# Two graph attention layers: the factor row made in every partition, and the turned tiles moved ahead in the second layer

## The chip, the cores and the metric

The kernel runs on one core of a Trainium2 chip. The metric is the device time of one execution in microseconds (us); the time before is the median of three runs. All data and all matmuls are float32.

## What is computed

For each of 8 graphs with 1024 nodes and 128 features, two layers run one after the other, each on the layer-normalised input behind a relu:

```python
h = relu(layernorm(x)); x = x + gat0(h)        # gat0 ends in elu
h = relu(layernorm(x)); x = x + gat1(h)        # gat1 has no elu
# gat: Wh = h @ W; e[i, j] = leaky_relu(Wh[i] @ a1 + Wh[j] @ a2, 0.2)
#      softmax over j where adj[i, j], then the sum of softmax * Wh[j]
```

The kernel uses that the leaky relu's exponential is a product and a maximum: with c the largest `Wh @ a2` of the graph, the weight of the pair (i, j) is the larger of a factor of j alone and a factor r of i alone, up to factors that cancel in the softmax. r is exp(-0.8 * max(Wh[i] @ a1 + c, 0)). So every partition (a node j) needs the row r of all 1024 nodes i, and every graph needs its c.

## The kernel before, in words

There are 16 **stages**: stage n is layer n // 8 and graph n % 8, and the program's constant LAST is 15. A graph has T = 8 tiles of 128 nodes. The loop over n (L1090 on TensorE, L841 on VectorE, L553 on ScalarE, L296 on the DMA queue of SyncE) overlaps three stages: it attends stage n, projects stage n+1 and makes the normalised input of stage n+2. Each engine has its order written out by hand, and semaphores bind them. Turn n of the loop finishes stage n-1; "a turn with elu" is one where stage n-1 is of the first layer, n = 1 to 8, and turns 9 to 14 are without elu.

**TensorE** in turn n: `project(n + 1)` is 8 matmuls, 16 instructions (a float32 matmul is two). In even turns `usum_pair` adds two. `attend(n, ...)` is 8 tiles of 8 matmuls, 128 instructions. In the middle of tile 0 `spread_emax` (L974) sends one transpose: the largest e2 of each partition (`emax`) is turned so that each partition gets all 128 of them. `transposes(n + 2)` (L900) turns the eight normalised tiles `xn`, 8 instructions, ahead of tile 6 in a turn with elu and of tile 5 in the others.

**VectorE** in turn n: the first two masks (`masks`, L734, 1024 columns, one per tile of attend), `take_acc(n - 1)` (three copies of the sums out of PSUM and a reciprocal `rec`), `copy_e(n + 1)` (L673: e1 and e2 out of the projection, then `emax`), a mask and `exp_args` in this order, or the other in turns without elu (L695: c as `cmax`, then `zrow` = max(e1 + c, 0) and `from_max` = e2 - c), the masks up to 5, `add_elu` or `add_hp`, masks 6 and 7, `statistics(n + 3)`. The masks of the next turn wait for the row `row_r` of the next stage.

**ScalarE**: `exps(n + 1)` (r, the two factors q and s, and the column of q in `wh`), `scale_accs(n - 1)` (8 instructions), `elu_exp` where there is an elu, `normalise(n + 2)` (8 instructions into `xn`), `scale_wh(n + 1)` (8), `sort_row(n + 1)` (L478: the row in the order that the masks want), `copy_hT(n + 2)` (L437). In even turns `copy_u` (L487) copies two rows of sums. TensorE's next `project` waits for all of `scale_wh` and for `copy_hT`.

**SyncE's queue**: `load_row(n + 1)` (L251) waits for r, writes it to `row_mem` in DRAM, waits for the landing, and reads it back into all 128 partitions (`in_row`). In odd stages the two rows `u_sums` travel with it. Behind it in the same queue stand the adjacency loads (1 MB each), the loads of x and the stores.

**GpSimd** has the statistics of the normalisation (`centre`, `variance`, `normaliser`) and nothing else in the loop.

Of the kernel before, what the change touches and what calls it, by code (L numbers as in the profile page):

```python
# [5 lines left out]
P = 128  # L6
# [6 lines left out]
SLOPE = 0.2  # L13
# [5 lines left out]
def gat_two_layers(nc, x, adj, w0, w0t, a0, w1, w1t, a1, r_rows, out):  # L19
# [27 lines left out]


# [6 lines left out]
    with ExitStack() as ctx:  # L55
# [36 lines left out]
        ecol = sb("ecol", [P, T, 2])  # L92
        emax = sb("emax", [P, 1])
# [6 lines left out]
        in_row = sb("in_row", [P, N + 2 * C])  # L100
        row_by_node = in_row[:, 0:N]
        u_rows = in_row[:, N:N + 2 * C].rearrange("p (s c) -> p s c", s=2)
# [16 lines left out]
        row_mem = nc.dram_tensor("row_mem", (N + 2 * C,), F32, kind="Internal").ap()  # L119
# [56 lines left out]
        q_ready = sem("q_ready")  # L176
        row_sorted = sem("row_sorted")
# [42 lines left out]

        def written(m):

            return loaded_rows(m) + (m - 1) // 2
# [14 lines left out]
        def _(sp):  # L238
# [11 lines left out]

            def load_row(m):  # L251
                k = loaded_rows(m)
                if m % 2 == 1:

                    sp.wait_ge(u_copied, m // 2)
                    sp.wait_ge(row_in, 16 * (k - 1))
                    sp.dma_start(row_mem[N:N + 2 * C].rearrange("(s c) -> s c", s=2),
                                 u_sums[:, :]).then_inc(r_written, 16)

                sp.wait_ge(r_known, m + 1)  # L260
                if k > 1:
                    sp.wait_ge(row_in, 16 * (k - 1))
                sp.dma_start(row_mem[0:N].rearrange("(p t) -> p t", t=T),
                             sqr[:, m % 2, 2, :]).then_inc(r_written, 16)
                sp.wait_ge(r_written, 16 * written(m))
                if k > 1:
                    sp.wait_ge(row_sorted, k - 1)

                sp.wait_ge(acc_copied, NB * (m - 1))
                if m % 2 == 0:  # L270
                    sp.dma_start(row_by_node, row_mem[0:N].partition_broadcast(P)
                                 ).then_inc(row_in, 16)
                else:
                    sp.dma_start(in_row[:, :], row_mem.partition_broadcast(P)).then_inc(row_in, 16)
# [42 lines left out]
        def _(pool):  # L317
# [34 lines left out]

            nc.gpsimd.memset(ident[:, :], 0.0).then_inc(const_set, 1)
# [14 lines left out]
            for m in range(1, LAST + 1):  # L368
                if m != 2:
                    centre(m)  # L370
                    variance(m)
                normaliser(m)

        @block.scalar
        def _(act):
# [71 lines left out]
            def exps(m):  # L447

                act.wait_ge(z_ready, m + 1)
                nc.scalar.activation(sqr[:, m % 2, 2, :], zrow[:, :], ACT.Exp,  # L450
                                     scale=SLOPE - 1.0).then_inc(r_known, 1)
                act.wait_ge(args_ready, m + 1)
                nc.scalar.activation(sqr[:, m % 2, 1, :], from_max[:, :], ACT.Exp,
                                     scale=SLOPE).then_inc(q_known, 1)
                nc.scalar.activation(sqr[:, m % 2, 0, :], from_max[:, :], ACT.Exp,
                                     scale=1.0 - SLOPE).then_inc(sqr_ready, 1)
                if m > 0:
                    act.wait_ge(q_known, m + 1)
                    nc.scalar.mul(wh[:, m % 2, :, D], sqr[:, m % 2, 1, :],
                                  Q_SCALE).then_inc(q_ready, 1)  # L460

# [16 lines left out]
            def sort_row(m):  # L478

                k = loaded_rows(m)  # L480
                act.wait_ge(row_in, 16 * k)
                act.wait_ge(p_ready, T * (m - 1))
                nc.scalar.activation(row_r[:, m % 2, :].rearrange("q (t p) -> q t p", t=T),  # L483
                                     row_by_node[:, :].rearrange("q (p t) -> q t p", t=T),
                                     ACT.Copy).then_inc(row_sorted, 1)

            def copy_u(n):  # L487
                k = n // 2
                act.wait_ge(upair_done, k)
                if k > 1:  # L490
                    act.wait_ge(r_written, 16 * written(n - 1))
                nc.scalar.activation(u_sums[:, 0:D], UPAIR, ACT.Copy,  # L492
                                     scale=EMPTY).then_inc(u_copied, 1)
# [59 lines left out]
            for n in range(1, LAST + 1):  # L553
                elu = stages[n - 1][0] == 0
                if n == LAST:
                    seed_last()
                if n < LAST and not elu:
                    if n % 2 == 0:
                        copy_u(n)
                    exps(n + 1)  # L560
                scale_accs(n - 1)
                if n < LAST:
                    if elu:
                        if n % 2 == 0:
                            copy_u(n)
                        exps(n + 1)
# [5 lines left out]
                    early = T // 2 if elu else T  # L572
                    scale_wh(n + 1, range(early))
                    sort_row(n + 1)
                    if early < T:
                        scale_wh(n + 1, range(early, T))
                if n + 2 <= LAST:
                    copy_hT(n + 2)

        @block.vector  # L580
        def _(dve):
# [103 lines left out]

            def exp_args_first():
# [8 lines left out]
            def exp_args(m):  # L695
                dve.wait_ge(emax_spread, m + 1)
# [41 lines left out]
            def mask_unsorted(n):  # L738
# [6 lines left out]
                    row_by_node[:, :].rearrange("q (p t) -> q t p", t=T),  # L745
# [95 lines left out]
            for n in range(1, LAST):  # L841
# [3 lines left out]
                copy_e(n + 1)  # L845
                if l == 0:
                    masks(n, (DRAIN,))
                    exp_args(n + 1)
                else:

                    exp_args(n + 1)
                    masks(n, (DRAIN,))
                masks(n, range(DRAIN + 1, 6))
# [19 lines left out]
        def _(pe):  # L873
# [26 lines left out]
            def transposes(m):  # L900
# [5 lines left out]
                else:  # L906
                    pe.wait_ge(cmax_ready, m)
# [82 lines left out]
            def spread_r(m):  # L990
                pe.wait_ge(r_known, m + 1)
# [98 lines left out]
            for n in range(1, LAST):  # L1090
# [4 lines left out]
                k = 6 if stages[n - 1][0] == 0 else 5  # L1095
                attend(n, (0,), emax_of=n + 1)
# [37 lines left out]
```

## Time and profile before

| what | value |
|---|---|
| median of 3 runs | 290.97 us (290.93 to 291.45) |
| the profiled execution | 291.18 us |
| its span, first to last instruction | 289.4 us |
| TensorE busy | 285.1 us (99%) |
| VectorE busy | 254.4 us (88%) |
| ScalarE busy | 195.1 us (67%) |
| GpSimd busy | 79.7 us (28%) |
| HBM traffic | 291 GB/s over the span |

The span leaves out some 1.8 us around the program. An engine is busy while one of its instructions runs; TensorE's instructions overlap each other, so that the distance from one start to the next tells more than their length. A row of the timeline has start, length, engine, line, operation, tiles, count, and in brackets the idle time ahead of it and who ended it.

### The profile page before, as it was taken

Reading aid. Unit: us, or ns where it says so; the run is one execution under the profiler, and the core shown is the slowest. Engines: PE = TensorE matmul, PEld = TensorE weight load, DVE = VectorE, ACT = ScalarE, POOL = GpSimd, SP = SyncE. Lnnn points to the kernel's source line nnn. Section 1 sums busy time; section 2 is a strip of 40 time slices with the busy share of each in tenths; the row PEclk is TensorE's granted clock in tenths of the full one; section 3 lists DMA queues with packets and bytes.
Section 4 is the critical chain, followed back from the end, with each engine's and each line's share of the span. In section 5 each row is a group of like instructions: output and inputs, shape, how many; then the busy total and the mean of one; then the engine's idle time right before and its main releaser. Section 6 shows DMA issues by size and latency. Waiting matters only on the chain.

```text
span 289.4 us, 6600 instructions
## 1 busy us (share of the span) xinstructions
PE 285.1 (99%) x2523; PEld 284.2 (98%) x2523; DVE 254.4 (88%) x493; ACT 195.1 (67%) x534; POOL 79.7 (28%) x143
## 2 busy tenths in 40 slices
PE   7999999999999999999999999999999999999996
PEld 7999999999999999999999999999999999999995
DVE  3898899898989989898998979979797997779986
ACT  4686795995959679495886929569292865916400
POOL 2412705315071420706035070512407042000000
PEclk9999999999999999999999999999999999999999
DMA  7999659597795949679287896959769596896922
GB/s 235 418 407 407 243 183 408 216 371 298 260 413 163 415 170 359 278 245 412 76 315 286 291 378 204 404 186 389 294 243 410 166 409 250 313 406 205 374 104 75
DMA packets 25387, 84.52 MB, mean 292 GB/s; under 512 B 3966, under 2 KB 5132, under 8 KB 25356
## 3 DMA queue, kind: packets, MB, share of 16 engines
q1 hardware_dynamic: 24780, 83.70, 76.8%
q8 instruction: 20, 0.33, 0.4%
q10 hardware_dynamic: 576, 0.39, 0.4%
q14 instruction: 11, 0.09, 0.1%
HBM read 79.83 MB, written 4.26 MB: 291 GB/s over the span
## 4 chain that ended last, share of the span: by engine, by line
PE 99%; POOL 0%; DVE 0%; issue 0%; POOLq 0%
PE acc L1041 76%; PE prj L957 9%; PE tp L887 5%; PE acc L1056 2%; PE acc L876 2%; PE acc L937 1%; PE tp L976 1%; PE prj L1056 1%; PE prj L927 1%; PE prj L1041 1%; PE tp L970 1%; PE tp L896 0%; PE tp L993 0%; PE tp L985 0%; PE acc L896 0%
## 5 line engine op out<-in xcount | busy, mean ns | idle before, releaser
L1041 PE MATMUL acc<-wh,pbuf 128*128 128x129 f32 x1968 | 227.6, 275 | 0.0
L1041 PEld LDWEIGHTS acc<-wh,pbuf 128*128 128x128 f32 x1968 | 224.0, 192 | 0.1
L734 DVE SCALAR_TENSOR_TENSOR pbuf<-row_r,sqr,adj_sb 128x1024 f32<-128x1024 f32 x125 | 154.8, 1277 | 2.9 <-ACT row_r L483 2.9
L498 ACT ACTIVATE accs<-accs,rec 128x128 f32<-128x128 f32 x120 | 36.6, 388 | 26.7 <-DVE rec L770 26.7
L320 POOL TENSOR_TENSOR mean<-stats 128x8 f32<-128x8 f32 x14 | 11.7, 836 | 142.9 <-DVE stats L632 139.5
L433 ACT ACTIVATE xn<-x_sb,shift,rstd 128x128 f32<-128x128 f32 x120 | 47.7, 479 | 0.0
L466 ACT ACTIVATE wh<-prj,wh 128x128 f32<-128x128 f32 x120 | 32.8, 363 | 0.0
L483 ACT ACTIVATE row_r<-in_row 128x1024 f32<-128x1024 f32 x14 | 29.4, 2098 | 2.4 <-DMA in_row<-row_mem 2.4
L957 PE MATMUL prj<-w_ext,hT 128*128 128x130 f32 x240 | 29.3, 275 | 0.0
L957 PEld LDWEIGHTS prj<-w_ext,hT 128*128 128x128 f32 x240 | 28.0, 191 | 0.0
L347 POOL TENSOR_TENSOR rstd<-vareps,neg_half 128x8 f32<-128x8 f32 x15 | 26.0, 1731 | 6.9 <-DVE vareps L651 5.8
L632 DVE BATCH_NORM_STATS2 stats<-x_sb 128x6 f32<-128x128 f32 x112 | 23.0, 278 | 0.0
L450 ACT ACTIVATE sqr<-zrow 128x8 f32<-128x8 f32 x16 | 3.3, 209 | 27.3 <-DVE zrow L699 26.9
L760 DVE TENSOR_TENSOR accs<-acc,in_row 128x387 f32<-128x387 f32 (+1 forms) x39 | 18.7, 512 | 0.6 <-PE acc L1041 0.2
L676 DVE COPY ecol<-prj 128x12 f32<-128x12 f32 x15 | 2.6, 171 | 16.1 <-PE prj L957 15.4
L323 POOL TENSOR_SCALAR negmean<-mean 128x8 f32<-128x8 f32 x14 | 15.6, 1112 | 1.2
L444 ACT ACTIVATE hT<-tp 128x1024 f32<-128x1024 f32 x15 | 15.5, 1033 | 0.6 <-PE tp L887 0.6
L887 PE MATMUL tp<-ident,xn 128*128 128x128 f32 x120 | 15.6, 273 | 0.0
L887 PEld LDWEIGHTS tp<-ident,xn 128*128 128x128 f32 x120 | 13.6, 141 | 0.0
L492 ACT ACTIVATE u_sums<-tp 2x128 f32<-2x128 f32 x7 | 1.8, 257 | 13.8 <-PE tp L970 13.8
L781 DVE TENSOR_TENSOR x_sb<-x_sb,ex 128x1024 f32<-128x1024 f32 x8 | 9.7, 1217 | 0.0
L775 DVE SCALAR_TENSOR_TENSOR ex<-accs,ex 128x1024 f32<-128x1024 f32 x8 | 9.7, 1217 | 0.0
(114 smaller groups left out, 181.1 us busy)
## 6 DMA issues: line engine op xcount, KB each, us to landing
adj_sb<-in_adj SPq DMA_DIRECT2D x64, 1024.0 KB, 10.7
in_row<-row_mem SPq DMA_DIRECT2D x7, 641.0 KB, 4.3
x_sb<-in_x SPq DMA_DIRECT2D x7, 512.0 KB, 11.5
in_row<-row_mem SPq DMA_DIRECT2D x7, 512.0 KB, 4.3
out_x<-x_sb SPq DMA_DIRECT2D x7, 512.0 KB, 12.9
x_sb<-in_x ACTq DMA_DIRECT2D x1, 256.0 KB, 3.6
x_sb<-in_x SPq DMA_DIRECT2D x1, 256.0 KB, 3.5
row_mem<-sqr SPq DMA_DIRECT2D x14, 4.0 KB
```

Of the source, the lines that this page charges most:

```text
L323: nc.gpsimd.tensor_scalar(negmean[:, :], mean2[:, :], -0.5, None, ALU.mult).then_inc(pool_means, 1)
L347: nc.gpsimd.tensor_tensor(rstd[:, :], vareps[:, :], neg_half[:, :], ALU.pow).then_inc(rstd_ready, 1)
L433: nc.scalar.activation(xn[:, t, :], src[:, t, :], ACT.Identity, bias=shift[:, t:t + 1], scale=rstd[:, t:t + 1]).then_inc(xn_ready, 1)
L466: nc.scalar.activation(wh[:, m % 2, t, 0:D], prj[:, k, s * E:s * E + D], ACT.Copy, scale=wh[:, m % 2, t, D:C]).then_inc(wh_ready, 1)
L483: nc.scalar.activation(row_r[:, m % 2, :].rearrange("q (t p) -> q t p", t=T), row_by_node[:, :].rearrange("q (p t) -> q t p", t=T), ACT.Co ...
L498: op = nc.scalar.activation(hp[:, t, :], hp[:, t, :], ACT.Copy, scale=rec[:, t:t + 1])
L632: st = nc.vector.bn_stats(stats[:, t, :], src[:, t, :])
L734: nc.vector.scalar_tensor_tensor(pbuf[:, t, :], row_r[:, n % 2, :], sqr[:, n % 2, 0, t:t + 1], adj_at(n, t), ALU.max, ALU.min).then_inc(p_ ...
L760: nc.vector.tensor_tensor(accs[:, k * NB:k * NB + w, :], acc[:, k, 0:w * C].rearrange("p (s c) -> p s c", c=C), uniform_of(e).unsqueeze(1) ...
L887: return nc.tensor.transpose(tp[:, t * P:(t + 1) * P], xn[:, t, :], ident[:, :])
L957: mm = nc.tensor.matmul(prj[:, k, s * E:(s + 1) * E], hT[:, t * P:(t + 1) * P], w_ext[:, l, :], start=(s == 0), stop=True, skip_group_chec ...
L1041: mm = nc.tensor.matmul(sum_at(k, s), pbuf[:, t, i * P:(i + 1) * P], wh[:, n % 2, t, :], start=(t == 0 and s == 0 and k < NB), stop=(t == ...
```

## The change

In stages 2 to 14 the row r is no longer made once and sent: e1 of all nodes and each partition's largest e2 travel through DRAM together, nine numbers a partition instead of eight (`e_row`, a row of 1152 instead of 1024 numbers in `row_mem` and `in_row`). They leave as soon as `emax` is made. Every partition then takes c from its own copy (`exp_args_later`) and makes r for all 1024 nodes itself (`make_row`: a relu with c as its bias, then an exponential in place). c is taken ahead of mask 6 in turns with elu, ahead of mask 7 in the others. `spread_emax` stays for stages 0, 1 and 15 (`OWN_R`). The column of q moves from ScalarE to GpSimd (`last_column`), `copy_u` from ScalarE to VectorE. In turns without elu `transposes` moves from ahead of tile 5 to ahead of tile 3, and `copy_hT` from the end of ScalarE's turn to right behind `normalise`. The diff, cut to its core:

```diff
+    OWN_R = (0, 1, LAST)
+        e_pair = sb("e_pair", [P, 2, T + 1])
+        e_row = e_pair[:, 0, :]
+        e2 = e_pair[:, 1, 0:T]
+        ROW = N + P
+        row_parts = in_row[:, 0:ROW].rearrange("q (p t) -> q t p", t=T + 1)
...
             def load_row(m):
+                if m in OWN_R:
...
+                else:
+                    sp.wait_ge(emax_ready, m + 1)
+                    sp.dma_start(row_mem[0:ROW].rearrange("(p t) -> p t", t=T + 1),
+                                 e_row).then_inc(r_written, 16)
+                    if m % 2 == 1:
+                        store_uniform(m)
...
+            def last_column(m):
+                pool.wait_ge(q_known, m + 1)
+                nc.gpsimd.tensor_scalar(wh[:, m % 2, :, D], sqr[:, m % 2, 1, :], Q_SCALE, None,
+                                        ALU.mult).then_inc(q_ready, 1)
...
                 normaliser(m)
+                if m > 2:
+                    last_column(m - 1)
...
+            def make_row(m):
+                k = loaded_rows(m)
+                act.wait_ge(row_in, 16 * k)
+                act.wait_ge(cmax_ready, m + 1)
+                act.wait_ge(p_ready, T * (m - 1))
+                nc.scalar.activation(row_r[:, m % 2, :].rearrange("q (t p) -> q t p", t=T),
+                                     row_parts[:, 0:T, :], ACT.Relu,
+                                     bias=cmax[:, 0:1]).then_inc(row_added, 1)
+                act.wait_ge(row_added, k)
+                nc.scalar.activation(row_r[:, m % 2, :], row_r[:, m % 2, :], ACT.Exp,
+                                     scale=SLOPE - 1.0).then_inc(row_sorted, 1)
...
                     if n + 2 <= LAST:
                         normalise(n + 2)
+                        if not elu:
+                            copy_hT(n + 2)
+                    if n + 1 == LAST:
+                        scale_wh(n + 1)
+                        sort_row(n + 1)
+                    else:
+                        exps_later(n + 1)
+                        make_row(n + 1)
+                        scale_wh(n + 1)
-                if n + 2 <= LAST:
+                if n + 2 <= LAST and elu:
                     copy_hT(n + 2)
...
+            def exp_args_later(m):
+                dve.wait_ge(row_in, 16 * loaded_rows(m))
+                nc.vector.tensor_reduce(cmax[:, :], row_parts[:, T, :], AX_X,
+                                        ALU.max).then_inc(cmax_ready, 1)
+                dve.wait_ge(cmax_ready, m + 1)
+                nc.vector.tensor_scalar(from_max[:, :], e2, cmax[:, 0:1], None,
+                                        ALU.subtract).then_inc(args_ready, 1)
...
+                masks(n, range(DRAIN, 6))
                 if l == 0:
                     add_elu(b)
+                    exp_args_later(n + 1)
                     masks(n, (6,))
                     add_x(b)
                     masks(n, (7,))
                 else:
                     add_hp(b)
-                    masks(n, (6, 7))
+                    masks(n, (6,))
+                    if n + 1 < LAST:
+                        exp_args_later(n + 1)
+                    masks(n, (7,))
...
-                else:
-                    pe.wait_ge(cmax_ready, m)
                 pe.wait_ge(xn_ready, xn_before(m + 1))
...
-                k = 6 if stages[n - 1][0] == 0 else 5
-                attend(n, (0,), emax_of=n + 1)
+                k = 6 if stages[n - 1][0] == 0 else 3
+                attend(n, (0,), emax_of=n + 1 if n + 1 == LAST else None)
```

`copy_e_later` is `copy_e` with e1 and e2 in separate rows, so that e1 and the maximum lie together; `exps_later` is `exps` without r and without the column.

## Rows read from the trace of the kernel before

**Rows 1.** The page, part 1: busy time and share of TensorE.

```profile
PE 285.1 (99%) x2523; PEld 284.2 (98%) x2523; DVE 254.4 (88%) x493; ACT 195.1 (67%) x534; POOL 79.7 (28%) x143
```

**Rows 2.** The page, part 4: the chain of waits, share by engine.

```profile
PE 99%; POOL 0%; DVE 0%; issue 0%; POOLq 0%
```

**Rows 3.** Timeline of TensorE: turn 3 from its first instruction to turn 4's.

```profile
66.83 1.95 PE L957 MATMUL prj<-w_ext,hT 128*128 128x130 f32 x16
...
69.51 0.27 PE L976 MATMUL tp<-ident,emax 128*128 128x128 f32 x1
...
83.89 1.95 PE L957 MATMUL prj<-w_ext,hT 128*128 128x130 f32 x16
```

**Rows 4.** Timeline of turn 3 (with elu): VectorE, ScalarE and the DMA queue.

```profile
68.82 0.17 DVE L676 COPY ecol<-prj 128x12 f32<-128x12 f32 x1 [1.10 <-PE prj L957]
69.09 0.16 DVE L684 TENSOR_REDUCE emax<-ecol 128x1 f32<-128x8 f32 x1
...
70.36 0.28 DVE L697 TENSOR_REDUCE cmax<-tp 128x1 f32<-128x128 f32 x1
...
70.96 3.67 DVE L734 SCALAR_TENSOR_TENSOR pbuf<-row_r,sqr,adj_sb 128x1024 f32<-128x1024 f32 x3
...
71.18 0.34 SPq L263 DMA_DIRECT2D row_mem<-sqr  x1
...
72.93 0.34 SPq L271 DMA_DIRECT2D in_row<-row_mem  x1
...
74.55 1.21 DVE L775 SCALAR_TENSOR_TENSOR ex<-accs,ex 128x1024 f32<-128x1024 f32 x1
...
75.69 1.27 DVE L734 SCALAR_TENSOR_TENSOR pbuf<-row_r,sqr,adj_sb 128x1024 f32<-128x1024 f32 x1
...
80.63 1.06 ACT L444 ACTIVATE hT<-tp 128x1024 f32<-128x1024 f32 x1
...
81.54 0.25 ACT L444 ACTIVATION_READ_ACCUMULATOR hT<-tp 128x1 f32 x1
...
84.58 0.20 DVE L770 RECIPROCAL rec<-accs 128x8 f32<-128x8 f32 x1
```

**Rows 5.** Lines by form: line, operation, count, busy us, mean ns, idle before.

```profile
L483 ACT ACTIVATE row_r<-in_row 128x1024 f32<-128x1024 f32 x14 | 29.4, 2098 | 2.4 <-DMA in_row<-row_mem 2.4
...
L323 POOL TENSOR_SCALAR negmean<-mean 128x8 f32<-128x8 f32 x14 | 15.6, 1112 | 1.2
...
L510 ACT ACTIVATE ex<-ex 128x1024 f32<-128x1024 f32 x8 | 8.5, 1058 | 0.3
...
L453 ACT ACTIVATE sqr<-from_max 128x8 f32<-128x8 f32 x16 | 3.3, 209 | 0.0
```

**Rows 6.** The tile in_row: time from issue to landing of its reads.

```profile
DMA to landing us min/median/max: 3.6/4.3/4.5
```

**Rows 7.** Timeline of turn 11 (without elu), ScalarE and VectorE.

```profile
208.31 2.44 ACT L498 ACTIVATE accs<-accs,rec 128x128 f32<-128x128 f32 x8
...
210.75 3.18 ACT L433 ACTIVATE xn<-x_sb,shift,rstd 128x128 f32<-128x128 f32 x8
...
213.83 2.12 ACT L466 ACTIVATE wh<-prj,wh 128x128 f32<-128x128 f32 x8
...
218.04 2.48 DVE L734 SCALAR_TENSOR_TENSOR pbuf<-row_r,sqr,adj_sb 128x1024 f32<-128x1024 f32 x2 [0.25 <-ACT row_r L483]
...
221.99 0.20 DVE L770 RECIPROCAL rec<-accs 128x8 f32<-128x8 f32 x1
```

**Rows 8.** Timeline of the DMA queue: the row's write and read, turn 8.

```profile
156.95 0.35 SPq L263 DMA_DIRECT2D row_mem<-sqr  x1
...
159.21 0.33 SPq L274 DMA_DIRECT2D in_row<-row_mem  x1
```

**Rows 9.** The same in turn 13.

```profile
242.41 0.34 SPq L263 DMA_DIRECT2D row_mem<-sqr  x1
...
245.67 0.32 SPq L271 DMA_DIRECT2D in_row<-row_mem  x1
```

More of the change, by code:

```diff
@@ L98, in gat_two_layers @@
         row_r = sb("row_r", [P, 2, N])
[L100 to L102 removed]
+        ROW = N + P
+        in_row = sb("in_row", [P, ROW + 2 * C])
+        row_parts = in_row[:, 0:ROW].rearrange("q (p t) -> q t p", t=T + 1)
+        u_rows = in_row[:, ROW:ROW + 2 * C].rearrange("p (s c) -> p s c", s=2)
         uniform = sb("uniform", [P, 2, C])
@@ L219, in e_copies, with own_rows @@
             return 3 * m + 3 if m < 2 else 2 * m + 4
+        def own_rows(m):
+            return len([k for k in OWN_R if k < m])
         def written(m):
@@ L270, in load_row @@
                 if m % 2 == 0:
-                    sp.dma_start(row_by_node, row_mem[0:N].partition_broadcast(P)
+                    sp.dma_start(in_row[:, 0:ROW], row_mem[0:ROW].partition_broadcast(P)
                                  ).then_inc(row_in, 16)
@@ L460, in exps, with exps_later @@
                                   Q_SCALE).then_inc(q_ready, 1)
+            def exps_later(m):
+                act.wait_ge(args_ready, m + 1)
+                nc.scalar.activation(sqr[:, m % 2, 1, :], from_max[:, :], ACT.Exp,
+                                     scale=SLOPE).then_inc(q_known, 1)
+                nc.scalar.activation(sqr[:, m % 2, 0, :], from_max[:, :], ACT.Exp,
+                                     scale=1.0 - SLOPE).then_inc(sqr_ready, 1)
             def scale_wh(m, tiles=range(T)):
@@ L556, in _ @@
                     seed_last()
-                if n < LAST and not elu:
-                    if n % 2 == 0:
-                        copy_u(n)
+                if n + 1 == LAST:
                     exps(n + 1)
@@ L569, in _ @@
                         normalise(n + 2)
[L572 to L576, printed above, removed]
-                if n + 2 <= LAST:
+                        if not elu:
+                            copy_hT(n + 2)
+                    if n + 1 == LAST:
+                        scale_wh(n + 1)
[5 more added lines that the diff above has]
+                if n + 2 <= LAST and elu:
                     copy_hT(n + 2)
@@ L684, in copy_e, with copy_e_later, copy_u @@
                 nc.vector.tensor_reduce(emax[:, :], ecol[:, :, 1], AX_X, ALU.max).then_inc(emax_ready, 1)
+            def copy_e_later(m):
+                dve.wait_ge(prj_done, m + 1)
+                full = prj[:, 0:2, 0:NB * E].rearrange("p b (s e) -> p b s e", e=E)[:, :, :, D:E]
+                nc.vector.tensor_copy(e_pair[:, :, 0:2 * NB].rearrange("p e (b s) -> p b s e", b=2),
+                                      full).then_inc(e_copied, 1)
+                part = prj[:, 2, 0:tiles_in[2] * E].rearrange("p (s e) -> p s e", e=E)[:, :, D:E]
+                nc.vector.tensor_copy(e_pair[:, :, 2 * NB:T].rearrange("p e t -> p t e"),
+                                      part).then_inc(e_copied, 1)
+                dve.wait_ge(e_copied, e_copies(m))
+                nc.vector.tensor_reduce(e_row[:, T:T + 1], e2, AX_X,
+                                        ALU.max).then_inc(emax_ready, 1)
+            def copy_u(n):
+                k = n // 2
+                dve.wait_ge(upair_done, k)
+                if k > 1:
+                    dve.wait_ge(r_written, 16 * written(n - 1))
+                nc.vector.tensor_scalar(u_sums[:, 0:D], UPAIR, EMPTY, None,
+                                        ALU.mult).then_inc(u_copied, 1)
             def exp_args_first():
@@ L844, in _ @@
                 take_acc(n - 1)
-                copy_e(n + 1)
-                if l == 0:
-                    masks(n, (DRAIN,))
+                if n + 1 == LAST:
+                    copy_e(n + 1)
+                else:
+                    copy_e_later(n + 1)
+                if n % 2 == 0:
+                    copy_u(n)
+                if n + 1 == LAST:
                     exp_args(n + 1)
-                else:
-                    exp_args(n + 1)
-                    masks(n, (DRAIN,))
-                masks(n, range(DRAIN + 1, 6))
+                masks(n, range(DRAIN, 6))
                 if l == 0:
                     add_elu(b)
+                    exp_args_later(n + 1)
                     masks(n, (6,))
```

40 lines of the change are left out of this document (15 added, 25 removed).

## The prediction

> **What bounds the kernel now.** I read the busy shares first: TensorE is busy for 99% of the span, VectorE for 88% [rows 1]. The chain of waits says the same: 99% of what ended last is TensorE [rows 2]. Busy time of overlapping matmuls proves little, so the timeline of TensorE comes next. From the first instruction of turn 3 to that of turn 4 are 17.06 us [rows 3]. The code issues 153 instructions in it: 16 of project, 128 of attend, 8 transposes, 1 of spread_emax. That is 0.1115 us for each, and the view shows no idle time anywhere in the turn. So TensorE issues back to back: an instruction less is time less, and any wait that reaches it is time more. What the other engines have left is read from rows 4: VectorE waits 1.10 us for the projection in this turn and for nothing else, and ScalarE has hT ready at 81.79 (81.54 + 0.25), 2.1 us ahead of the project that needs it.
>
> **The change on TensorE.** One transpose goes in each of the turns 1 to 13: 13 x 0.1115 = 1.45 us. Moving the eight others from tile 5 to tile 3 changes no count. If nothing else reaches TensorE, the profiled execution goes from 291.18 to 289.73, and the median, which stands 0.21 below it, from 290.97 to 289.52. A turn is then 16.95 us, or 17.17 with the two instructions of usum_pair. The Trainium skill, page "TensorE: Matmul & The Clock Gate", section "Back-to-back issue gap", gives some 81 ns for a matmul with 128 columns; by it the 13 would be worth an estimated 1.05 us. The row's 0.1115 decides, since it is this kernel's own spacing.
>
> **The row's way, with elu.** I count from T, the first instruction of a turn (66.83 in turn 3). In turn 3 emax is done at 69.25, T + 2.42 [rows 4]. The write left at 71.18, behind the spread, three VectorE operations and an exponential. Now it leaves at T + 2.42, 1.93 us earlier. From the write to the read's issue are 1.75 us in turn 3 [rows 4], and the read lands 4.3 us after its issue [rows 6]. So the row is there at T + 8.47. The broadcast carries 64 KB more on its 512 or 641 KB; both old sizes have the same median to landing, so I add nothing. The adjacency loads stand behind the row in the same queue and start earlier by as much; their buffers have been free for a turn.
>
> VectorE comes to exp_args_later when add_elu is issued out. It began add_elu at 74.55; without the three operations between 70.36 and 70.96 that is 73.95, and 1.14 us later (74.55 to 75.69) it would begin mask 6 [rows 4]: 75.09, T + 8.26. So c is taken at about T + 8.5, after a wait of 0.2. In even turns copy_u lies ahead of it; a read of 128 columns from PSUM took 0.28 (the old cmax) [rows 4], which I take for it, with 0.16 (the emax reduce) as its lower end.
>
> ScalarE after c: the reduce and from_max fit in the 0.60 that three operations took; two exponentials of 8 columns at 0.21 [rows 5]; the relu; the exponential; scale_wh at 2.12 [rows 7]; copy_hT at 1.16 (80.63 to 81.79) [rows 4]. For the relu there is the sort at 2.10, which reads the same row with a step of 32 bytes, and a contiguous relu of 1024 columns at 1.06 [rows 5]. The new step is 36 bytes, so I take 2.10. No row shows a step of 36; twice the strided price is my upper end. The exponential in place is contiguous: 1.06. Together 0.60 + 0.42 + 2.10 + 1.06 + 2.12 + 1.16 = 7.46, hT at T + 15.96. The next project starts at T + 16.95: 1.0 us in hand, where there were 2.1. With a contiguous price there would be 2.0, at the upper end none and a stall of 1.1 in each of eight turns.
>
> VectorE after c: from mask 6 to the end of rec took 9.09 (75.69 to 84.78) [rows 4], so rec is done 9.6 after c, at T + 18.1 or 1.15 into the next turn. It must be done by 1.99 into it (68.82 - 66.83), when copy_e can begin: 0.8 in hand.
>
> **The column of q** on GpSimd: eight columns, between ScalarE's 0.21 and GpSimd's dearest such row, 1.11 [rows 5]. It is needed 3 us later by scale_wh, behind make_row, so it costs nothing; were make_row not there, scale_wh would wait for it. GpSimd itself waits for the exponentials in that place; behind it stand only the next statistics, which come at the end of VectorE's turn.
>
> **Turns without elu.** c is taken after mask 6, 1.2 us later, at T + 9.46. The row lands at T + 2.42 + 4.3 plus its write: with the longest write shown, 3.26 us in turn 13 [rows 9], T + 9.98. scale_wh ends 6.3 after c, at T + 16.3 at worst, still ahead of the project. make_row ends 4.2 after c, T + 13.66; the next masks began at 218.04, T + 13.8, held by the same row [rows 7]. So rec keeps its place, 0.89 into a turn (222.19). From there scale_accs and normalise take 5.62 (208.31 to 213.93) [rows 7], so xn is whole 6.6 into the turn. TensorE comes to the turned tiles after 64 instructions, 7.14. The move to tile 3 holds with 0.5 us, and copy_hT then fills ScalarE's wait for c.
>
> **Where it gets tight** is turn 9, the first without elu behind one with it. In turn 8 the write took 2.26 us [rows 8], and u_sums is issued one issue (0.34) behind. The row lands at T + 2.42 + 0.34 + 2.26 + 4.3 = T + 9.3, rec ends 9.6 later, 1.8 into turn 9, xn is whole at 7.4, and TensorE wants it at 7.14: a stall of 0.3 us. With a write of 1.75 there is none; with the slowest landing and copy_u at its upper end 0.8. Turn 14 keeps the old way, and copy_u ahead of exp_args delays its row by 0.28; I charge nothing, as the last turn sends no turned tiles. SyncE issues no more DMAs than before.
>
> **The sum**: 290.97 - 1.45 + 0.3 = 289.8 us, with 289.5 and 290.3 for stalls of none and 0.8.
>
> **Rivals.** First, the row becomes a loop that sets the pace. c of a turn with elu comes 0.43 + write + 4.3 after copy_e begins, and 9.6 later the next copy_e can begin: 14.3 + write, 0.34 more in even turns, against 17.06 on average. Up to a write of 2.55 us it hides; above that VectorE, held in exp_args_later with masks 6 and 7 queued behind it, comes later in each turn, and TensorE waits for masks, hT and turned tiles. At 3.26 in all eight turns it is 0.7 each, less the 0.8 in hand: 4.8 us, so 294.3. It cancels the gain from about 2.84. For it: 2.26 and 3.26 stand in the trace, and this wait had 2 us of cover before. Against it: 1.75 in turn 3, and the long one is in the second layer, which has room. The Trainium skill, page "DMA: Bandwidth & Descriptors", section "Latency and other measured facts", puts a DRAM access at 0.2 us on average and 2 us under high load and makes it most of a DMA's fixed cost; by that the writes would be late where adjacency loads still run. The spread of these rows fits it, though they do not show its cause. Chance 0.18.
>
> Second, the turned tiles stall TensorE in all the turns 9 to 13. With slow landings the 0.5 us is gone: 0.8 in turn 9 and up to 0.4 in four more, 2.4 in all; half of it, 1.2, gives 290.7, no change that can be told. Chance 0.15.
>
> Third, the change removes nothing that counted, since each spread's place is filled by some other wait, as VectorE's. Then it is 291.0. Against it: VectorE has 1.10 us idle in the turn [rows 4] and gains only 0.15. Chance 0.03.
>
> **The numbers.** The forecast (289.5 to 290.3) has 0.64. A measurement of this kernel can tell about 0.2%, 0.58 us: faster is below 290.39, slower above 291.55. Faster: the forecast, and a part of the second case, 0.67. Slower: the first case and a share of the strided relu's upper end, 0.18. Within: 0.15. The range 289.3 to 291.6 holds the forecast, the second and third case and the mild end of the first.
>
> **What would show it.** Right: 13 rows of spread_emax gone, a turn with elu at 16.95 us, TensorE without idle time but for a few tenths at the turned tiles of turn 9; the write of the row at T + 2.4; relu 2.1 and exponential 1.05 in make_row; a VectorE wait for in_row of some tenths a turn. Wrong: idle time of TensorE ahead of project (hT or wh late), ahead of masks' matmuls, or ahead of the turned tiles of every turn from 9 on; a wait of VectorE for in_row of 1 us and more; turns with elu longer than 17.1.

## The result and the profile after

The changed kernel takes 295.71 us (median of 5 runs, 295.13 to 297.11); the kernel before took 290.97 beside it. The ratio is 1.0166 (95% interval 1.014 to 1.0192): it is slower by 4.74 us, where 1.2 us less was forecast. A few executions of the runs below came out far longer than the others of their kernel (759 us in e1, 303.43 and 305.70 in e3, 308.81 in e4); ratios leave them out, and so do the medians given here.

The profiled execution took 297.11 us with a span of 295.3. TensorE's turn 1 starts at 33.87, 1.39 us later than before, ahead of all that the change touches in the loop. That is of this one execution, which lies 1.40 above the median: in the other profiled runs with the change, e1 aside, turn 1 starts at 32.00 to 32.54. From the start of turn 1 to that of turn 14 are 227.64 us (33.87 to 261.51), against 223.18 before (32.48 to 255.66): 4.46 more. That is where the time lies. The page of the changed kernel, part 1 and the first lines of part 4:

```profile
PE 286.0 (97%) x2510; PEld 283.8 (96%) x2510; DVE 254.5 (86%) x487; ACT 207.0 (70%) x514; POOL 110.2 (37%) x156
...
PE 52%; POOL 14%; ACT 13%; DVE 11%; DMA 6%; issue 3%; SPq 0%; DVEq 0%; ACTq 0%; POOLq 0%
PE acc L1113 36%; POOL shift L372 8%; PE prj L1029 7%; DVE pbuf L804 6%; ACT xn L463 4%; ACT row_r L532 4%; DMA in_row<-row_mem 3%; ACT wh L504 3%; POOL rstd L369 2%; PE tp L961 2%; DVE stats L674 2%; PE acc L1128 2%; POOL mean L342 2%; POOL negmean L345 2%; DMA row_mem<-e_pair 1%
```

TensorE has its 13 instructions less (2510 against 2523), but it holds 52% of the chain where it held 99% [rows 2]. A single GpSimd line, `shift` (L372), has 8%; the diff doesn't touch it. GpSimd is busy for 110.2 us, 30.5 more than [rows 1]: `last_column` is only 12.3 of them, and `shift`, which took 7.2 in all before, takes 26.0. The waits of the changed kernel (who waited for whom, us in total, times, longest):

```profile
ACT act_gate L460 <- POOL shift L372: 13.4, 5, 3.1
...
DVE cmax L768 <- DMA in_row<-row_mem: 6.6, 8, 1.6
```

and of TensorE alone:

```profile
PE prj L1029 <- ACT hT L474: 4.5, 4, 1.2
```

TensorE waits four times ahead of `project`, at the ends of turns 2, 4, 6 and 8, for 1.10 to 1.15 us. The stretch from turn 2's first instruction (50.82) to turn 3's (69.26) shows the way there. Timeline of the changed kernel:

```profile
51.85 1.67 POOL L369 TENSOR_TENSOR rstd<-vareps,neg_half 128x8 f32<-128x8 f32 x1
...
53.16 0.27 DVE L745 TENSOR_SCALAR u_sums<-tp 2x128 f32<-2x128 f32 x1
53.32 0.34 SPq L283 DMA_DIRECT2D row_mem<-e_pair  x1
53.36 4.85 DVE L804 SCALAR_TENSOR_TENSOR pbuf<-row_r,sqr,adj_sb 128x1024 f32<-128x1024 f32 x4
53.59 5.82 POOL L372 TENSOR_TENSOR shift<-negmean,rstd 128x8 f32<-128x8 f32 x1
...
55.17 0.34 SPq L296 DMA_DIRECT2D in_row<-row_mem  x1
...
58.14 1.20 DVE L845 SCALAR_TENSOR_TENSOR ex<-accs,ex 128x1024 f32<-128x1024 f32 x1
59.51 0.20 ACT L460 ACTIVATE act_gate<-shift 128x1 f32<-128x1 f32 x1 [2.84 <-POOL shift L372]
...
59.62 3.18 ACT L463 ACTIVATE xn<-x_sb,shift,rstd 128x128 f32<-128x128 f32 x8
59.80 0.39 DVE L768 TENSOR_REDUCE cmax<-in_row 128x1 f32<-128x128 f32 x1 [0.46 <-DMA in_row<-row_mem]
...
62.90 2.16 ACT L532 ACTIVATE row_r<-in_row,cmax 128x1024 f32<-128x1024 f32 x1
...
65.08 1.06 ACT L536 ACTIVATE row_r<-row_r 128x1024 f32<-128x1024 f32 x1
...
68.95 0.26 ACT L474 ACTIVATION_READ_ACCUMULATOR hT<-tp 128x1 f32 x1
...
69.26 0.49 PE L1029 MATMUL prj<-w_ext,hT 128*128 128x130 f32 x2 [1.10 <-ACT hT L474]
```

`shift` multiplies eight columns. It starts at 53.59, within mask 2, and ends at 59.41, as `add_elu` does (59.34): masks 2 to 5 and `add_elu` stand behind `copy_u` (L745) without a gap. `normalise` waits for it until 59.51, make_row, scale_wh and copy_hT stand behind `normalise` on ScalarE, and hT is done at 69.21, 18.39 into the turn where 15.96 was forecast. In turns 2, 4, 6 and 8 `shift` takes 5.82, 4.91, 6.09 and 6.10 us. In the odd turns, which have no `copy_u`, it takes 0.20 (0.95 in turn 5); in the kernel before 1.22 in turns 2, 4, 6 and 8 and 0.20 in the others. Timelines of VectorE and GpSimd, first in turn 2 of the kernel before, where `shift` ends with the one mask that it met:

```profile
51.88 1.28 DVE L734 SCALAR_TENSOR_TENSOR pbuf<-row_r,sqr,adj_sb 128x1024 f32<-128x1024 f32 x1
...
53.08 0.28 DVE L697 TENSOR_REDUCE cmax<-tp 128x1 f32<-128x128 f32 x1
...
52.00 1.22 POOL L350 TENSOR_TENSOR shift<-negmean,rstd 128x8 f32<-128x8 f32 x1
```

then in turn 5 of the changed kernel, where it ends with mask 2 as well, though three more masks and `add_elu` follow without a gap:

```profile
107.26 4.87 DVE L804 SCALAR_TENSOR_TENSOR pbuf<-row_r,sqr,adj_sb 128x1024 f32<-128x1024 f32 x4
...
107.64 0.95 POOL L372 TENSOR_TENSOR shift<-negmean,rstd 128x8 f32<-128x8 f32 x1
```

By the starts of TensorE's turns: turns 2, 4, 6 and 8 take 18.44, 18.49, 18.46 and 18.46, together 5.17 more than four times 17.17; the odd turns behind them 17.06 each, 0.11 more than 16.95, since `project` took 2.05 behind the wait instead of the 1.95 of [rows 3]; turns 12 and 13 have 0.16 and 0.20 more. In all that is 5.97 lost; less the 1.45 that the transposes were to save, 4.52, where 4.46 was measured.

### The profile page after: what moved, and what is told of

It reads as the page before. It is cut to its first block, busy times and chain, and to the rows that moved or that the text cites. A ratio compares the mean times of both kernels' runs of the same rounds, so it can differ in the third digit from the quotient of the medians.

```text
span 295.3 us, 6553 instructions
## 1 busy us (share of the span) xinstructions
PE 286.0 (97%) x2510; PEld 283.8 (96%) x2510; DVE 254.5 (86%) x487; ACT 207.0 (70%) x514; POOL 110.2 (37%) x156
## 4 chain that ended last, share of the span: by engine, by line
PE 52%; POOL 14%; ACT 13%; DVE 11%; DMA 6%; issue 3%; SPq 0%; DVEq 0%; ACTq 0%; POOLq 0%
PE acc L1113 36%; POOL shift L372 8%; PE prj L1029 7%; DVE pbuf L804 6%; ACT xn L463 4%; ACT row_r L532 4%; DMA in_row<-row_mem 3%; ACT wh L504 3%; POOL rstd L369 2%; PE tp L961 2%; DVE stats L674 2%; PE acc L1128 2%; POOL mean L342 2%; POOL negmean L345 2%; DMA row_mem<-e_pair 1%
## 5 line engine op out<-in xcount | busy, mean ns | idle before, releaser
L378 POOL TENSOR_SCALAR wh<-sqr 128x8 f32<-128x8 f32 x13 | 12.3, 947 | 89.3 <-ACT sqr L495 89.3
L532 ACT ACTIVATE row_r<-in_row,cmax 128x1024 f32<-128x1024 f32 x13 | 28.1, 2165 | 0.1
L372 POOL TENSOR_TENSOR shift<-negmean,rstd 128x8 f32<-128x8 f32 x15 | 26.0, 1730 | 1.2
L342 POOL TENSOR_TENSOR mean<-stats 128x8 f32<-128x8 f32 x14 | 8.8, 627 | 39.4 <-DVE stats L674 34.5
L474 ACT ACTIVATE hT<-tp 128x1024 f32<-128x1024 f32 x15 | 15.8, 1050 | 8.2 <-PE tp L961 8.2
L536 ACT ACTIVATE row_r<-row_r 128x1024 f32<-128x1024 f32 x13 | 13.7, 1057 | 0.4
L460 ACT ACTIVATE act_gate<-shift 128x1 f32<-128x1 f32 x15 | 2.9, 193 | 13.4 <-POOL shift L372 13.4
L731 DVE COPY e_pair<-prj 128x12 f32<-128x12 f32 x13 | 2.3, 177 | 11.0 <-PE prj L1029 11.0
L768 DVE TENSOR_REDUCE cmax<-in_row 128x1 f32<-128x128 f32 x13 | 5.0, 382 | 6.6 <-DMA in_row<-row_mem 6.6
```

Source lines behind the costliest of these rows:

```text
L372: nc.gpsimd.tensor_tensor(shift[:, :], negmean[:, :], rstd[:, :], ALU.mult).then_inc(shift_ready, 1)
```

## The experiments

My theory after the result (the lock, from here on): VectorE's operations keep GpSimd's `shift` out for as long as they follow one another without a break (the series), and the change joined them, since `exp_args` no longer stands behind mask 2 and `copy_u` now stands ahead of it. The first rival: the row's way has become a loop that paces VectorE (the prediction's first rival). Each edit is against the changed kernel, where nothing else is said. Ratios are to the kernel before in the same series. "Write to read" is the time between the two issues of the row on SyncE's queue.

**e1, e5: VectorE waits for shift ahead of mask 2, in every turn.**

```diff
+                if n + 2 <= LAST:
+                    dve.wait_ge(shift_ready, n + 2)
                 masks(n, range(DRAIN, 6))
```

> VectorE waits for GpSimd's shift ahead of mask 2 in every turn, so that shift never meets a running mask. Lock theory (GpSimd's shift cannot run while VectorE runs masks 2 to 5 and add_elu in an unbroken series; it is late in the even turns with elu, ScalarE's normalise waits for it and hT comes 1.2 us late): shift takes 0.2 us in all turns instead of 4.9 to 6.1 in four, xn is whole 9 us into an even turn instead of 12, the four stalls of TensorE of about 1.25 us ahead of project go, 5.0 in all: 295.7 goes to 290.3 to 291.0. Loop theory (the round trip of the row sets the pace): the stalls stay, 295.5 to 296.5.

291.98 us, 1.0036 (1.0022 to 1.0051). Most of the loss is gone, but it isn't faster than before. The profile is of the 759-us execution and tells nothing of the turns, so the same kernel ran again:

> The kernel with the wait for shift ahead of mask 2 once more, for its profile: its times came to 1.0036 of the kernel before, 1.05 us above it, where 1.45 below was to be had, so some 2.5 us of stalls are left. Row theory (the rest is the row that lands late): stalls ahead of project or of the turned tiles only in turns whose row's write took over 2.4 us (turns 3, 4 and 11 to 13), each with a wait of VectorE for in_row in the same turn or the one ahead; shift 0.2 us everywhere. The other theory (VectorE lost time in its new wait): every even turn is 17.3 us or more whatever the row does. 291.7 to 292.4.

292.67 us, 1.0063 (1.0038 to 1.0088). `shift` takes 0.20 in every turn and no 1.1-us stall is left. The wait brings its own loop: `shift` starts 2.11, 2.77, 2.97, 3.55, 3.82 and 3.92 us into turns 1 to 6, and turns 5 to 9 take 17.27, 17.39, 17.53, 17.28 and 17.82. VectorE's waits in e5:

```profile
DVE pbuf L804 <- POOL shift L372: 9.5, 8, 1.5
```

The masks wait for `shift`, `shift` for the statistics, and these stand behind the masks: each turn hands its delay on.

**e2, e3: a one-column memset on VectorE** after mask 2, or after mask 4.

```diff
-                masks(n, range(DRAIN, 6))
+                masks(n, range(DRAIN, 3))
+                nc.vector.memset(gate[:, :], 0.0)
+                masks(n, range(3, 6))
```

> One memset of one column (59 ns, no input) on VectorE behind mask 2 of every turn, nothing else. Lock theory, if any instruction without two inputs from SBUF opens the way: shift of the even turns 2, 4, 6 and 8 ends with mask 2, about 3.9 into the turn (it took 4.9 to 6.1 us and ends at 8.6), a length of 1.2 to 1.5 us, and the time is that of a wait for shift, 290.3 to 291.0. If the gap is too short for it, shift stays at 5 to 6 us. Loop theory: 295.7 either way.

295.63 us, 1.0161 (1.0142 to 1.018); `shift` 5.86, 4.96, 6.09 and 6.09.

> The same memset, two masks later, behind mask 4. Lock theory: shift of the even turns with elu ends with mask 4, about 6.3 into the turn, a length of 3.6 to 3.9 us; normalise, which could start at 5.9, is held by 0.4 to 0.6, and the stalls are gone all the same or below 0.2 us: within 0.5 us of the run with the gap behind mask 2. Loop theory: 295.7.

296.41 and 297.32 us in the two executions that the ratio is from, 1.0202 (1.0181 to 1.0223); `shift` 5.92, 4.91, 6.02 and 6.10. A memset in the series, if it comes without a pause, opens nothing.

**e4: c after mask 6 instead of ahead of it**, in turns with elu: one mask more in the series.

```diff
                     add_elu(b)
-                    exp_args_later(n + 1)
                     masks(n, (6,))
+                    exp_args_later(n + 1)
```

> In turns with elu c is taken behind mask 6, 1.2 us later than in the changed kernel, so that the row has that much longer to land; the series of VectorE instructions that shift meets is longer by that mask. Lock theory: shift of turns 2, 4, 6 and 8 takes 6 to 7.3 us, their stalls grow from 1.25 to about 2.5 us: 4 to 5 us slower, 299 to 301. Loop theory: VectorE's waits for in_row (6.6 us in eight waits) fall to under 2 us and the time with them: 292 to 294.

301.06 us, 1.0333 (1.0307 to 1.0359). `shift` takes 7.29 to 7.32 in the four turns: one mask longer, as the series, and the turns 19.61 to 19.66. `shift` takes as long as the series does. In the profiled execution VectorE waited 2.23 us for the row in turn 11; in turn 12 `shift` began 2.56 into the turn, 0.06 ahead of mask 2, and took 7.31 there too: an even turn without elu locks as well once `shift` comes late. There the lock is dearer, since the turned tiles stand early in the turn. Timelines of GpSimd and TensorE in that turn:

```profile
233.98 7.31 POOL L372 TENSOR_TENSOR shift<-negmean,rstd 128x8 f32<-128x8 f32 x1
...
244.72 1.54 PE L961 MATMUL tp<-ident,xn 128*128 128x128 f32 x6 [5.70 <-ACT xn L463]
```

TensorE waited 5.70 us for the tiles; its granted clock, 1.00 ahead of the wait, was 0.50 (1.2 GHz) from 243 to 248 and 1.00 again from 250 on, and the turn took 24.93. In the profiled execution of e3 turn 12 has the same: `shift` 7.32, a wait of 5.71, 25.91 in all. So these two executions are long by the lock itself. The row's loop, which gave 292 to 294, falls as the cause.

**e6, e7: no adjacency loads in stages 3 to 15**, with the wait of e1 (e6) and without it (e7): `load_adj` returns at once for them.

> The same, and the adjacency loads of stages 3 to 15 left out, so that those stages use the adjacency of the first three; all other work is the same. The row then meets no traffic but x and the stores. Row theory: the row's write takes 1.4 to 1.6 us in every turn, no stall is left, turns are 16.95 and 17.17: 289.4 to 289.8. If VectorE's own work is the rest: 291.5 to 292.

291.61 us, 1.0015 (0.9993 to 1.0038). Turns 10 to 13 are whole again, but turns 6 to 9 take 17.29, 17.54, 17.28 and 17.82, much as in e5: that drift is the wait's own.

> The changed kernel with the same adjacency loads left out, without the wait for shift. Lock theory: the four stalls of turns 2, 4, 6 and 8 stay, 1.25 each, and shift takes 5 to 6 us in them: 289.5 + 5.0 = 294.0 to 294.8. Loop theory (all was the row): 289.4 to 290.

295.18 us, 1.0137 (1.012 to 1.0154): the four turns still take 18.45 to 18.46, `shift` 6.10, 4.91, 6.10 and 5.63. The four stalls need no adjacency traffic.

**e8: the kernel before, with exp_args after mask 3** in turns with elu. `masks(n, (DRAIN,))` became `masks(n, (DRAIN, DRAIN + 1))`.

> The kernel before with exp_args one mask later in turns with elu, behind mask 3 instead of mask 2. Lock theory: shift of turns 2, 4, 6 and 8, which began under mask 2 and ended with it after 1.22 us, now ends with mask 3 after 2.4 to 2.5; it is 0.2 in the odd turns still. The row leaves 1.2 us later: 291 to 292. If shift's length has another cause: 1.22 as before.

291.43 us in one run. `shift` ends with mask 2, 3.68 us into the turn, not with mask 3. Timelines of VectorE and GpSimd in e8, turn 2 (49.69):

```profile
52.03 2.47 DVE L734 SCALAR_TENSOR_TENSOR pbuf<-row_r,sqr,adj_sb 128x1024 f32<-128x1024 f32 x2
...
52.47 0.90 POOL L350 TENSOR_TENSOR shift<-negmean,rstd 128x8 f32<-128x8 f32 x1
```

So a series alone doesn't hold GpSimd: it gets on at the end of the one mask that it met. My theory lacked a part, and `copy_u` is what e8 lacks.

**e9: copy_u ahead of the reduce that makes emax**, so that it no longer stands right ahead of the masks.

> The changed kernel with copy_u one place earlier on VectorE, ahead of the reduce into emax instead of behind it, so that the masks follow the reduce in every turn, as they do in odd turns. What the runs so far show: a GpSimd instruction that meets a mask gets on at the end of that mask, but behind copy_u it waits for the whole series. If copy_u right ahead of the masks is what shuts GpSimd out: shift of the even turns takes at most 1.4 us and ends with mask 2, about 3.9 into the turn, no stall of 1.25 is left: 290.0 to 291.2 (emax is 0.28 later in even turns). If it is the unbroken series alone: shift stays at 5 to 6 us, 295 to 296.

294.89 us, 1.0109 (1.0083 to 1.0135); `shift` 6.03, 5.53 and 5.97 in turns 2, 6 and 8. A whole-width operation between `copy_u` and mask 2 doesn't help. In turn 4 `shift` came late, when mask 2 had ended, and took 1.23. Timelines of VectorE and GpSimd in e9, turn 4 (85.02):

```profile
87.37 0.27 DVE L747 TENSOR_SCALAR u_sums<-tp 2x128 f32<-2x128 f32 x1
87.57 0.14 DVE L739 TENSOR_REDUCE e_pair<-e_pair 128x1 f32<-128x8 f32 x1
87.64 4.85 DVE L806 SCALAR_TENSOR_TENSOR pbuf<-row_r,sqr,adj_sb 128x1024 f32<-128x1024 f32 x4
...
88.93 1.23 POOL L372 TENSOR_TENSOR shift<-negmean,rstd 128x8 f32<-128x8 f32 x1
```

**e10: copy_u on all 128 partitions.** It copies 126 rows more, which nobody reads; the DMA still takes two.

```diff
-        u_sums = sb("u_sums", [2, C])
+        u_sums = sb("u_sums", [P, C])
...
-                nc.vector.tensor_scalar(u_sums[:, 0:D], UPAIR, EMPTY, None,
+                nc.vector.tensor_scalar(u_sums[:, 0:D], tp[:, BANK:BANK + D], EMPTY, None,
```

> The changed kernel with copy_u on all 128 partitions instead of 2, same place, same length in columns. If it is the two-partition form that shuts GpSimd out: shift of the even turns at most 1.4 us, 290.0 to 291. If the instruction's place or kind does it: 5 to 6 us in turns 2, 4, 6, 8 and 295 to 296, as in the changed kernel.

290.60 us, 0.9974 (0.9955 to 0.9994). `shift` takes 0.20 to 1.29 everywhere. Timelines of e10 in turn 2 (49.12), to be held against turn 2 above:

```profile
51.47 0.28 DVE L745 TENSOR_SCALAR u_sums<-tp 128x128 f32<-128x128 f32 x1
51.67 4.86 DVE L804 SCALAR_TENSOR_TENSOR pbuf<-row_r,sqr,adj_sb 128x1024 f32<-128x1024 f32 x4
56.45 1.22 DVE L845 SCALAR_TENSOR_TENSOR ex<-accs,ex 128x1024 f32<-128x1024 f32 x1
...
51.71 1.29 POOL L372 TENSOR_TENSOR shift<-negmean,rstd 128x8 f32<-128x8 f32 x1
```

The same operations, the same length (0.28 against 0.27), the same place; only the partitions differ. `shift` ends at 53.00, with mask 2.

**e15: copy_u on 64 partitions.**

```diff
+                nc.vector.tensor_scalar(u_sums[0:64, 0:D], tp[0:64, BANK:BANK + D], EMPTY, None,
```

> The changed kernel with copy_u on 64 partitions where the change has 2 and the earlier version had 128. Theory that any VectorE operation on less than all partitions ahead of the masks shuts GpSimd out: shift takes 5 to 6 us in turns 2, 4, 6 and 8, these turns are 18.4 us, time 295 us. Rival, that it is the operation's length, or the two partitions alone, that does it: shift takes 1.3 us at most, time 290.4 to 290.9.

296.12 us, 1.0172 (1.0142 to 1.0201); timelines of e15 in turn 2 (49.29):

```profile
51.63 0.27 DVE L745 TENSOR_SCALAR u_sums<-tp 64x128 f32<-64x128 f32 x1
51.83 4.86 DVE L804 SCALAR_TENSOR_TENSOR pbuf<-row_r,sqr,adj_sb 128x1024 f32<-128x1024 f32 x4
...
51.95 5.93 POOL L372 TENSOR_TENSOR shift<-negmean,rstd 128x8 f32<-128x8 f32 x1
```

With 64 it locks as with 2; with 128 it doesn't. `u_sums` has 128 partitions here as in e10, so it is the operation's partitions that count and not the buffer's.

**e16: the kernel before, with copy_u on VectorE** behind copy_e, on two partitions, and nothing else of the change.

> The kernel before with one part of the change alone: copy_u moved from ScalarE to VectorE, on two partitions, between copy_e and the mask. There exp_args with its three short operations still stands between mask 2 and mask 3 in turns with elu. Theory that a VectorE operation on part of the partitions locks GpSimd out of an unbroken series only: shift begins in mask 2 and ends with it, 1.3 us at most as before, turns stay 17.29, time 290.8 to 291.8. Rival, that the two-partition copy_u alone shuts GpSimd out whatever follows: shift 4 to 6 us in turns 2, 4, 6 and 8, xn and hT later by as much, and time 292 us or more.

291.00 us, 0.9999 (0.9977 to 1.0022); `shift` 1.42 to 1.44 in turns 2, 4, 6 and 8, these turns 17.29.

**e17: e16 and e8 together**: copy_u on VectorE and exp_args after mask 3.

> The kernel before with copy_u on VectorE on two partitions and exp_args after mask 3 instead of after mask 2 in turns with elu (after mask 3 alone shift still ended with mask 2, 3.68 us into the turn). Theory that behind the partial copy_u the lock lasts to the end of the series: shift of turns 2, 4, 6 and 8 ends with mask 3, 4.9 to 5.1 us into the turn, 2 to 2.5 us long. Rival, that the length of the series after it doesn't matter: shift ends with mask 2, at 3.7 to 3.9, 1.3 us at most. A third case, that the lock passes exp_args too: shift ends after mask 5 or add_elu, 8 us or more into the turn.

291.07 us, 0.9986 (0.9964 to 1.0009). Timelines of e17 in turn 2 (49.32), the series and `shift`:

```profile
51.66 0.27 DVE L688 TENSOR_SCALAR u_sums<-tp 2x128 f32<-2x128 f32 x1
51.86 2.46 DVE L730 SCALAR_TENSOR_TENSOR pbuf<-row_r,sqr,adj_sb 128x1024 f32<-128x1024 f32 x2
54.25 0.27 DVE L693 TENSOR_REDUCE cmax<-tp 128x1 f32<-128x128 f32 x1
...
52.09 2.29 POOL L350 TENSOR_TENSOR shift<-negmean,rstd 128x8 f32<-128x8 f32 x1
```

Now `shift` ends at 54.38, with mask 3, in each of the four turns. In turns 3, 5 and 7 of the same kernel, which have the series but no `copy_u` ahead of it, it met mask 2 too and ended with that. Timelines of e17 in turn 3 (66.61):

```profile
68.95 2.47 DVE L730 SCALAR_TENSOR_TENSOR pbuf<-row_r,sqr,adj_sb 128x1024 f32<-128x1024 f32 x2
...
69.43 0.86 POOL L350 TENSOR_TENSOR shift<-negmean,rstd 128x8 f32<-128x8 f32 x1
```

In e8 it ended with mask 2; in e16 too, where `exp_args` stands behind that one. So neither the partial `copy_u` nor the series locks alone: behind the partial `copy_u`, `shift`, when it meets the first mask, stays out until the series ends.

**e11: copy_u back on ScalarE**, behind scale_accs.

> The changed kernel with copy_u back on ScalarE, behind scale_accs. Copy_u theory: shift at most 1.4 us everywhere and no stall of 1.25. u_sums leaves some 1.2 us later in even turns, so the row lands at 9 to 10 there and VectorE waits for it by up to 1.5 us: 290.3 to 292. Series theory: shift 5 to 6 us in even turns, 295 to 296.

294.56 us, 1.0105 (1.0067 to 1.0144). The lock is gone (`shift` 1.19 at most), and another loss is there: `u_sums` leaves later, and the row with it. VectorE's waits in e11:

```profile
DVE cmax L770 <- DMA in_row<-row_mem: 12.7, 10, 1.8
```

Turns 4 to 9 take 17.33, 17.06, 17.44, 17.30, 17.63 and 18.37, rec is done as late as 2.33 into a turn, and turn 9 stalls for the turned tiles (1.1 of it). That is the prediction's first rival and its turn 9, in one kernel: real once the row is later.

**e12: VectorE waits for shift ahead of mask 4**, as e1 but two masks later, in every turn.

> The changed kernel with VectorE's wait for shift two masks later than in the first run, ahead of mask 4 in turns with elu. In an odd turn shift is done by then; in an even one VectorE pauses for it at 5.0 and it is done at 5.2 to 5.3, ahead of normalise at 5.9. No stall of 1.25, and, unlike the wait ahead of mask 2, GpSimd's chain has 2 us of room, so that the turns do not drift: rec ends at 0.9 to 1.4 in all turns with elu, 290.0 to 291.0. If the drift has another cause than that wait: 292 to 292.7 again.

290.56 us, 0.9969 (0.9952 to 0.9986). `shift` takes 1.37 to 2.56 in the even turns with elu and ends with mask 3; there is no drift. With e10 it is the best of the versions that leave nothing out; both are about 0.3% faster than the kernel before.

**e13: e10 without the adjacency loads** of e7.

> The 128-partition copy_u with the adjacency loads of stages 3 to 15 left out (those stages mask with what the first loads put there). With all 128 partitions some turns were still longer than 16.95 or 17.17 (17.28 in turn 4, 17.42 in turn 12, 17.55 in turn 13), and in these the row's write-to-read took 2.98, 4.47 and 4.59 us. Theory that the row waits behind the adjacency traffic: write-to-read about 1.5 us in every turn, every turn at 16.95 or 17.18, time 289.3 to 289.8 us. Rival, that TensorE or VectorE loses these tenths for another reason: turns 4, 12 and 13 stay long and the time stays at 290.3 to 290.8.

290.22 us, 0.9962 (0.9942 to 0.9981). In the profiled execution (289.43) the turns 4, 12 and 13, which e10 has at 17.28, 17.42 and 17.55, take 17.18, 17.18 and 16.95; write to read in turns 12 and 13 is 1.53 and 1.42 instead of 4.47 and 4.59. These tenths are the row behind adjacency traffic. From turn 1 to turn 14 are 221.77 us, 1.41 less than before: the forecast's 1.45, when nothing else is lost. The median stands 0.8 above this execution, out of the expected range; the executions that made it up left no profile, so where they lose is open.

**e14: e10, with the load of x and an earlier store issued between the row's write and its read.**

> The 128-partition copy_u, with the load of x and the store of the stage before last issued between the row's write and its read, where the queue only waits. Theory that the row is slowed by the traffic that is under way when it is written: the x load and the store leave the rest of the queue, the adjacency loads start no earlier, and write-to-read stays as it was or shrinks in turns 11 to 13; time 289.6 to 290.3. Rival, that the two transfers only add to what the row waits behind: write-to-read grows by some tenths, time 290.6 to 291.5.

292.16 us (290.01 to 293.96), 1.0025 (1.0001 to 1.0049). In the profiled execution, the shortest of twelve, write to read fell to 1.53 to 2.00 in turns 10 to 13 as the theory wanted, but turn 3 took 17.38. The time rose, beyond the rival's guess. What the longer executions lose isn't shown; this is left open.

## Why the prediction was wrong

**TensorE: right.** Odd turns without a stall take 16.95 and even ones 17.17 to 17.18. Spread_emax is gone in 13 turns, and e13 shows the sum, 1.41 of 1.45. By the 81 ns that the Trainium skill has (page "TensorE: Matmul & The Clock Gate", section "Back-to-back issue gap") it would have been an estimated 1.05, which this trace does not bear out.

**The row's way and make_row: right in the pieces.** The row is written 2.45 to 2.60 into a turn (2.42 forecast). The groups of the changed kernel that answer to [rows 5] (busy us, mean ns, idle before):

```profile
L532 ACT ACTIVATE row_r<-in_row,cmax 128x1024 f32<-128x1024 f32 x13 | 28.1, 2165 | 0.1
...
L536 ACT ACTIVATE row_r<-row_r 128x1024 f32<-128x1024 f32 x13 | 13.7, 1057 | 0.4
...
L378 POOL TENSOR_SCALAR wh<-sqr 128x8 f32<-128x8 f32 x13 | 12.3, 947 | 89.3 <-ACT sqr L495 89.3
...
L768 DVE TENSOR_REDUCE cmax<-in_row 128x1 f32<-128x128 f32 x13 | 5.0, 382 | 6.6 <-DMA in_row<-row_mem 6.6
```

The relu took 2.165 (2.10 forecast), the exponential 1.057 (1.06). Where `shift` was not held up, hT was done 15.6 to 15.8 into the turn with an early row (15.96 forecast).

**The step that failed** is the one on GpSimd: "The column of q on GpSimd ... costs nothing ... GpSimd itself waits for the exponentials in that place; behind it stand only the next statistics", together with `copy_u` on VectorE priced at its own 0.28. Both prices hold: the column took 0.947, nobody waits for it, and `copy_u` took 0.27. What the step left out is GpSimd's work that the diff doesn't touch. `shift` had met mask 2 in the kernel before as well, and had ended with it. I counted the removal of `exp_args` from behind mask 2 as 0.6 us gained for VectorE and didn't ask what got on in that place, nor what an operation moved to VectorE does to the engine beside it. With one part of the edit alone the lock is not there (e16 has only the moved `copy_u`, e8 only a longer series), and with both, `shift` follows each: e10 changes the form of `copy_u`, e17 moves the end of the series.

How VectorE and GpSimd meet is also in the Trainium skill, page "SBUF — State Buffer", sections "SBUF: two separate sides" and "Who interferes with whom": a VectorE instruction with two SBUF inputs contends with a GpSimd instruction that reads SBUF, and the loser is blocked for the whole of the other's instruction. The kernel before, e8 and e16 agree (`shift` ended with the one mask it met). By this rule `shift` would have lost a mask's 1.2 us at most. The 5.82 us of turn 2 are five instructions; there the measurement decides. Why partial partitions make the difference, no run here shows.

**First rival (the row's loop, 294.3):** near in time, but not in cause; e4 and e7 refuted it for the changed kernel. Its mechanism exists: e11 pays it. Without the lock the median is 290.6 (e10, e12), 0.3 above the forecast's upper end; part of that is the late row: e13, without the adjacency loads, has 290.22. In the changed kernel the row was late in turns 3 and 4 (write to read 2.77 and 3.06, c waited 1.10 and 1.57), and the stall of turn 4 covered that (e10, without it, lost 0.04 and 0.10 in these turns).

**Second rival (turned tiles):** real in turns 12 and 13 alone, 0.16 and 0.20. There the row is the forecast's long one, and longer: 3.94 and 4.06 from write to read in turns 12 and 13, where [rows 9] had 3.26. The prediction had less in hand than it said: it let `make_row` end at 13.66, from c at 9.46, but with its own row at 9.98 that is 14.18, 0.4 behind the 13.8 at which the next masks began, which leaves 0.1 of the 0.5. **Turn 9's stall** of 0.3 did not come: rec was done 1.00 into the turn, since turn 8 was 1.3 longer. In e10, without that cover, xn is whole at 7.06 (7.4 forecast) and turn 9 takes 16.97.

**Signs named beforehand:** the idle time "ahead of project (hT or wh late)" and turns with elu "longer than 17.1" came; their cause was none of those priced.

## What to carry to other kernels

When an operation moves to VectorE, or a break between its long two-input operations goes, list what GpSimd does in that stretch, the untouched lines too, and who waits for it: here eight columns on GpSimd cost 5 us. (Tested is one pair: a tensor_scalar out of PSUM on VectorE and a tensor_tensor on GpSimd.) If a short VectorE operation on a few partitions stands ahead of such a series, give it all 128 partitions or end the series by a wait once the GpSimd work is due. And put that wait where the work is nearly done: two masks earlier the same wait made a loop (e1 and e5, 1.0036 and 1.0063, against e12, 0.9969).

## What the runs showed of the hardware

- Behind a VectorE tensor_scalar on 2 or 64 partitions a GpSimd tensor_tensor that met the first mask took 4.9 to 7.3 us, until the series of masks and what followed them without a break had ended; behind the same one on 128 partitions 0.20 to 1.29 (changed kernel, e4, e15; e10).
- It holds only what meets the first mask: in e9 the one `shift` that began in the second took 1.23. That is one case.
- A memset on VectorE between the masks doesn't end it (e2, e3: 4.91 to 6.10 in turns 2, 4, 6 and 8); a wait of VectorE (e12: 1.37 to 2.56) or a reduce out of PSUM (e17: 2.20 to 2.31) does.
- The row's write to read took 1.4 us in some turns and 4.6 in others of one kernel (e10); with the adjacency loads left out 1.4 to 1.5 in turns 9 to 13 (e13), but still 2.9 in turn 3.
